# Cross-attention and feed-forward block: both halves of a pair's scores follow each other, one projection bank fewer and keys in the outputs' bank

## The reference, cut to what matters

```python
lat, ctx = layer_norm(latents, ...), layer_norm(context, ...)
q = (lat @ Wq)                                  # [b, heads, 256, 64]
k, v = jnp.split(ctx @ Wkv, 2, axis=-1)         # [b, heads, 512, 64]
k = apply_rope(k, cos, sin)
attn = softmax(clip(q @ k.T * scale, -11, 11))
x = x + (attn @ v) @ Wo + bo
# second layer, per token
att = softmax(q2 (16x8) @ k2.T / sqrt(8)); out = att @ v2
x = x + (out @ Wo + bo); h2 = rmsnorm(x)
x = x + sum over e of softmax(h2 @ Wg + bg)[e] * (h2 @ We[e])
```

## Time and profile before

| what | us |
|---|---|
| three runs | 311.20, 311.25, 309.62 (median 311.2) |
| the profiled execution's own time | 310.52 |
| its span | 308.7 |
| TensorE matmul busy | 293.3 (95%) |
| TensorE weight loads busy | 205.2 (66%) |
| VectorE busy | 247.7 (80%) |
| GpSimd busy | 207.4 (67%) |
| ScalarE busy | 162.2 (53%) |
| mean granted TensorE clock | 0.991 |

### The profile page before, as it was taken

The page is one execution under the profiler, slowest core; times in us unless marked ns, Lnnn a source line. Parts: engine busy times, 40 slices in busy tenths (PEclk is TensorE's granted clock), DMA queues, the critical chain, the costliest instruction groups (busy, mean ns, idle before and its releaser), DMA issues.

```text
span 308.7 us, 6625 instructions
## 1 busy us (share of the span) xinstructions
PE 293.3 (95%) x2482; PEld 205.2 (66%) x2482; DVE 247.7 (80%) x452; ACT 162.2 (53%) x324; POOL 207.4 (67%) x209
## 2 busy tenths in 40 slices
PE   6889998999999999999999999999999999999983
PEld 6777665766678767566777676566787665576651
DVE  1896999966775869899889788977857699887875
ACT  2447555568551745664615555784436468514632
POOL 7255784556465738777665777499927588878763
PEclk9799999999999999999999999999999999999998
DMA  7463422221111111111111012011101100000001
GB/s 197 160 181 92 123 57 53 61 62 36 36 45 25 35 36 34 36 37 33 37 36 34 19 35 53 8 45 36 29 22 37 36 18 2 0 19 0 1 2 34
DMA packets 16319, 14.24 MB, mean 46 GB/s; under 512 B 4832, under 2 KB 11808, under 8 KB 16288
## 3 DMA queue, kind: packets, MB, share of 16 engines
q1 hardware_dynamic: 14992, 13.49, 16.9%
q10 hardware_dynamic: 1296, 0.33, 0.5%
HBM read 4.89 MB, written 0.52 MB: 18 GB/s over the span
## 4 chain that ended last, share of the span: by engine, by line
PE 64%; DVE 11%; POOL 8%; ACT 5%; issue 5%; DMA 4%; SPq 2%; POOLq 0%; ACTq 0%; DVEq 0%
PE pv L659 13%; PE sc L643 13%; PE sums L680 6%; PE pj_k L581 5%; PE pj_k L583 4%; PE pj_k L582 4%; PE side L767 4%; POOL moe L1944 2%; PE side L843 2%; POOL e L1870 2%; DMA sin_in<-in_L_xattn_sin_dram 2%; DMA kswap<-ksin 2%; SPq L548 2%; PE side L688 2%; ACT e L963 2%
## 5 line engine op out<-in xcount | busy, mean ns | idle before, releaser
L1870 POOL TENSOR_SCALAR e<-e 128x1024 f32<-128x1024 f32 x64 | 70.9, 1108 | 56.9 <-ACT e L963 46.4
L963 ACT ACTIVATE e<-sc 128x1024 f32<-128x1024 f32 x64 | 65.6, 1025 | 32.1 <-PE sc L643 31.7
L643 PEld LDWEIGHTS sc<-qs,ks 64*128 64x128 f32 x768 | 49.6, 185 | 21.8 <-issue 18.3
L643 PE MATMUL sc<-qs,ks 64*128 64x256 f32 x768 | 62.5, 295 | 0.5 <-ACT e L963 0.3
L659 PE MATMUL pv<-e,v 128*64 128x256 f32 x496 | 60.4, 385 | 0.6 <-POOL e L1870 0.4
L1863 POOL TENSOR_TENSOR krot<-kcos,kswap 128x512 f32<-128x512 f32 x32 | 43.7, 1365 | 11.8 <-DMA kswap<-ksin 9.3
L659 PEld LDWEIGHTS pv<-e,v 128*64 128x64 f32 x496 | 32.8, 136 | 21.5 <-issue 4.5
L971 ACT ACTIVATE u<-pv 128x256 f32<-128x256 f32 x31 | 11.9, 385 | 54.0 <-PE pv L659 47.9
L1321 DVE TENSOR_TENSOR ks<-krot,ks 128x512 fp32r<-128x512 f32 x32 | 32.1, 1004 | 0.1
L1385 DVE TENSOR_TENSOR ksin<-pj_k,sinT 128x512 f32<-128x512 f32 x32 | 21.9, 685 | 4.0 <-PE pj_k L583 3.8
L955 ACT ACTIVATE v<-pj_k 128x512 f32<-128x512 f32 x28 | 16.8, 599 | 15.1 <-PE pj_k L583 14.7
(11 more groups left out here) (304 smaller groups left out, 575.5 us busy)
## 6 DMA issues: line engine op xcount, KB each, us to landing
kswap<-ksin SPq DMA_DIRECT2D x126, 64.0 KB, 2.0
ctx_in<-in_ctx_dram SPq DMA_DIRECT2D x4, 256.0 KB, 4.1
prod<-in_L_xattn_Wkv_dram SPq DMA_DIRECT2D x2, 512.0 KB, 7.0
x_in<-in_x_dram SPq DMA_DIRECT2D x1, 512.0 KB, 6.6
prod<-in_L_xattn_Wq_dram SPq DMA_DIRECT2D x1, 512.0 KB, 7.4
wo<-in_L_xattn_Wo_dram SPq DMA_DIRECT2D x1, 512.0 KB, 4.4
fwe<-in_L_ffn_We_dram SPq DMA_DIRECT2D x1, 512.0 KB, 4.3
out_dram<-x_in SPq DMA_DIRECT2D x3, 128.0 KB, 1.9
```

The source lines that it names most:

```text
L643: last = nc.tensor.matmul(sc[:, h, c * NT:(c + 1) * NT], ks[rows, j % 3, k_part, chunk], qs[rows, j % 2, q_part, :], start=(k_part + q_par ...
L963: nc.scalar.activation(e[:, j % 3, :, 2 * half:2 * half + 2, :].rearrange("p h c n -> p h (c n)"), sc[:, :, :], ACT.Exp, scale=SCALE).then ...
L1870: nc.gpsimd.tensor_scalar(a, a, EXP_HIGH, EXP_LOW, ALU.min, ALU.max).then_inc(s_clip, 1)
```

## The change

- Each half of scores has two banks of its own, sc0 and sc1. The banks of sc1 also hold the projections: value units in its first, queries in its second. Keys go to pv, the outputs' bank.
- TensorE's slot becomes: both halves of scores, d, sums, outputs of slot-1, a, queries of slot+2, one value unit, b, keys of slot+3, c.
- The waits follow the banks. The second half of scores waits for the value unit's copy and the low part of the queries of slot+1; outputs wait until `key_products` has read the keys of three pairs on; keys wait for the copy of the outputs; queries and value units wait for the second exponential.
- ScalarE: both exponentials, `key_hi(slot+1)`, output copy, `query_hi(slot+2)`, value copy.
- VectorE: `query_lo(slot+1)`, `key_products(slot+2)`, the steps, `key_lo(slot+1)`, the rest, both `add_chunks`.
- GpSimd: both clips, then `rotate(slot+2)`.
- norm0 moves to the new place "d", lat_T from slot 6 "a" to slot 5 "b" of a batch; value units are spread as one for a slot.

```diff
...
+QUERIES_AHEAD = 2
...
 POST_STEPS = {
-    (1, "a"): "norm0", (1, "b"): "norm1", (1, "c"): "norm2", (2, "a"): "norm3", (2, "b"): "out_proj",
+    (1, "d"): "norm0", (1, "b"): "norm1", (1, "c"): "norm2", (2, "a"): "norm3", (2, "b"): "out_proj",
     (3, "c"): "h_T", (4, "a"): "query_down", (4, "b"): "keyval2", (10, "c"): "o_T", (11, "a"): "out_proj2",
     (12, "c"): "h2_T", (13, "a"): "gate", (14, "b"): "moe0", (14, "c"): "moe1", (15, "b"): "moe2",
     (16, "a"): "moe3",
...
-PREP_STEPS = {(3, "b"): "ctx_T", (6, "a"): "lat_T"}
+PREP_STEPS = {(3, "b"): "ctx_T", (5, "b"): "lat_T"}
...
 def value_units(slot):
     b, p = divmod(slot, PAIRS)
     if slot <= 0:
-        return [2, 3] if slot == 0 else []
-    if p >= PAIRS - 2 and b + 1 < NB:
-        first = 8 * (b + 1) + 2 * (p - (PAIRS - 2))
-        return [first, first + 1]
-    if 1 <= p <= 4 and 0 <= b < NB:
-        return [8 * b + 3 + p]
-    return []
...
+        return []
+    if p >= 5:
+        return [8 * (b + 1) + p - 5] if b + 1 < NB else []
+    return [8 * b + 3 + p] if b < NB and (p or b) else []
...
-        sc = es.enter_context(nc.psum_tensor("sc", [128, 2, 512], fp32))
-        sc_bank = [sc[:, h, :] for h in range(2)]
+        sc = [es.enter_context(nc.psum_tensor(f"sc{half}", [128, 2, 512], fp32)) for half in range(2)]
+        sc_bank = [sc[0][:, h, :] for h in range(2)]
+        pj_k = [sc[1][:, h, :] for h in range(2)]
         own_bank = pb("own_bank")
-        pj_k = [pb(f"pj_k{i}") for i in range(2)]
...
         def value_bank(n):
-            return first_value_banks[n] if value_units_at_first(n) else pj_k[PLACE["values", n] % 2]
+            return first_value_banks[n] if n < SC else pj_k[0]
         def key_bank(j):
-            return pj_k[PLACE["keys", j] % 2]
+            return (pj_k[0], sc_bank[0], sum_bank, pj_k[0])[j] if j <= KEYS_AHEAD else pv_bank
         def query_bank(j):
-            return pj_k[PLACE["queries", j] % 2]
+            return own_bank if j == 1 else pj_k[1]
...
-                bank_free("keys", j)
+                if j == KEYS_AHEAD:
+                    pe.wait_ge(s_exp, 2)
+                elif j > KEYS_AHEAD:
+                    pe.wait_ge(s_u, j - KEYS_AHEAD)
                 split3(key_bank(j)[:, :], wkA[:, 0, cols], wkA[:, 1, cols], ctxT[:, b % 2, 0, :],
...
-                bank_free("queries", j)
+                if j >= QUERIES_AHEAD:
+                    pe.wait_ge(s_exp, 2 * (j - QUERIES_AHEAD) + 2)
...
-                if not value_units_at_first(n):
-                    bank_free("values", n)
+                if n == 1:
+                    pe.wait_ge(s_kmul, 6)
+                if n >= SC:
+                    pe.wait_ge(s_exp, 2 * slot + 2)
                 elif n >= 2:
                     pe.wait_ge(s_v, n - 1)
...
                 if half == 0:
                     pe.wait_ge(s_klo, j + 1)
                     pe.wait_ge(s_qlo, j + 1)
-                if j or half:
-                    pe.wait_ge(s_exp, 2 * j + half)
+                    if j:
+                        pe.wait_ge(s_exp, 2 * j - 1)
+                    else:
+                        pe.wait_ge(s_kmul, 4)
+                else:
+                    if j:
+                        pe.wait_ge(s_exp, 2 * j)
+                    if j == 1:
+                        pe.wait_ge(s_kmul, 2 * KEYS_AHEAD + 2)
+                    for n in value_units(j - 1):
+                        pe.wait_ge(s_v, n + 1)
+                    if j and j - 1 + QUERIES_AHEAD < NPAIR:
+                        pe.wait_ge(s_qlo, j + QUERIES_AHEAD)
...
+                if KEYS_AHEAD < j + KEYS_AHEAD < NPAIR:
+                    pe.wait_ge(s_kmul, 2 * (j + KEYS_AHEAD) + 2)
...
+            for slot in range(NPAIR - 2):
+                scores(slot, 0)
+                scores(slot, 1)
+                side_at(slot, "d")
...
+                if PAIRS < slot and slot % 2 == 0:
+                    sums(slot - 1)
+                times_values(slot - 1)
+                if slot <= PAIRS and slot % 2 == 0:
+                    sums(slot - 1)
+                side_at(slot, "a")
+                if slot + QUERIES_AHEAD < NPAIR:
+                    queries(slot + QUERIES_AHEAD)
+                for n in value_units(slot):
+                    values(n, slot)
+                side_at(slot, "b")
                 if slot + KEYS_AHEAD < NPAIR:
-                    if slot != 0:
-                        keys(slot + KEYS_AHEAD)
-                    if slot == 1 - KEYS_AHEAD:
-                        keep_busy(WARM_UP["lat_T"], pv_bank)
-                        side_product("lat_T", 0)
-                    if slot == -1:
-                        keep_busy(WARM_UP["queries"], pv_bank)
-                elif slot + 1 < NPAIR:
-                    queries(slot + 1)
-                side_at(slot - 1, "c")
-                if queries_ahead(slot):
-                    queries(slot + 1)
-                if slot == 0:
-                    keep_busy(WARM_UP["scores"], pv_bank)
-                if 0 <= slot < NPAIR:
-                    scores(slot, 0)
-                if slot == 0:
-                    keys(KEYS_AHEAD)
-                if not after_outputs(slot):
-                    side_at(slot, "a")
-                if 0 <= slot + 1 < NPAIR and slot + KEYS_AHEAD < NPAIR and not queries_ahead(slot):
-                    queries(slot + 1)
-                if PAIRS < slot <= NPAIR and slot % 2 == 0:
-                    sums(slot - 1)
-                if 1 <= slot <= NPAIR:
-                    times_values(slot - 1)
-                if 2 <= slot <= PAIRS and slot % 2 == 0:
-                    sums(slot - 1)
-                if after_outputs(slot):
-                    side_at(slot, "a")
-                if slot == 0:
-                    values(0)
-                    values(1)
-                if 0 <= slot < NPAIR:
-                    scores(slot, 1)
-                side_at(slot, "b")
-                for n in value_units(slot):
-                    values(n)
+                    keys(slot + KEYS_AHEAD)
+                side_at(slot, "c")
...
-            for slot in range(-KEYS_AHEAD, NPAIR - 2):
+            key_hi(0)
...
+            for slot in range(NPAIR - 2):
                 side_taken(slot - 1, "c")
-                if 0 <= slot < NPAIR:
-                    exps(slot, 0)
-                side_taken(slot, "a")
-                if 0 <= slot + 1 < NPAIR:
-                    query_hi(slot + 1)
-                if 1 <= slot <= NPAIR:
+                exps(slot, 0)
+                exps(slot, 1)
...
+                    key_hi(slot + 1)
                     attention_copy(slot - 1)
...
-                    exps(slot, 1)
...
+                side_taken(slot, "a")
+                if slot + QUERIES_AHEAD < NPAIR:
+                    query_hi(slot + QUERIES_AHEAD)
+                for n in value_units(slot):
+                    value_copy(n)
                 if slot < NPAIR - 3:
                     side_taken(slot, "b")
-                for n in units:
-                    value_copy(n)
-                if 0 <= slot + KV_AHEAD < NPAIR:
-                    key_hi(slot + KV_AHEAD)
...
-            for slot in range(-KEYS_AHEAD, AFTER):
...
+            for slot in range(AFTER):
...
-                if 1 <= slot <= PAIRS:
-                    add_chunks(slot - 1, 1)
-                side_taken(slot - 1, "c")
-                if 2 <= slot + KEYS_AHEAD < NPAIR:
-                    key_products(slot + KEYS_AHEAD)
...
+                if slot + 1 < NPAIR:
                     query_lo(slot + 1)
+                if slot and slot + 2 < NPAIR:
+                    key_products(slot + 2)
+                side_taken(slot - 1, "c")
                 if more and p == 6:
                     split_latT(b + 1)
-                if after_outputs(slot):
-                    side_taken(slot, "a")
-                if 1 <= slot + 1 < NPAIR:
+                if more and p == 4:
+                    split_ctxT(b + 1)
+                second_layer(slot, "first")
+                side_taken(slot, "d")
+                second_layer(slot, "early")
+                side_taken(slot, "a")
+                if slot + 1 < NPAIR:
                     key_lo(slot + 1)
...
-                if 0 <= slot < PAIRS:
-                    add_chunks(slot, 0)
+                if slot < PAIRS:
+                    for half in range(2):
+                        add_chunks(slot, half)
...
+            for slot in range(AFTER):
...
-                if 0 <= slot + KV_AHEAD < NPAIR:
-                    rotate(slot + KV_AHEAD)
                 second_layer(slot, -1)
-                if 0 <= slot < NPAIR:
+                if slot < NPAIR:
                     clip(slot, 0)
                 second_layer(slot, 0)
-                if 0 <= slot < NPAIR:
+                if slot < NPAIR:
                     clip(slot, 1)
+                if slot + KV_AHEAD < NPAIR:
+                    rotate(slot + KV_AHEAD)
...
```

118 lines of the change are left out of this document (48 added, 70 removed).

## The result

The changed kernel takes **354.28 us** (median of four runs, 350.59 to 357.52), the kernel before on the same chip 310.41 (308.76 to 311.25): ratio 1.138, 95% interval 1.134 to 1.143. The prediction was 324.5 with a range of 309 to 336: the direction was right, the loss is three times as large. The profiled execution of the changed kernel took 357.52 us, its span is 355.7; it is the slowest of the four, 3.2 above the median, so sums read from its trace come out somewhat high.

A forecast was written before the change was run, and what follows sets the result against it. TensorE was taken to set the pace, with VectorE's lag harmless. 310.5 + (208.4 work + 32 new stalls - 224.4 before) - 2 at the ends = 324.5 us, 4% slower, range 309 to 336.

The forecast's parts named there:

- the repricing: TensorE, slots 1 to 29: uninterrupted work recounted with fewer changes of tile shape, 217.2 us before and 208.4 after.
- stalls, slots 1 to 9: New waits from statistics, normalising and added chunks behind the low keys, and reciprocals behind later sums: 3.7 us.
- The gain: TensorE: fewer shape changes save 8.9 us in slots 1 to 29; slot 0 gives 0.9 and the end 1.1.
- the gain is missing: Rival: on TensorE the pause between shapes returns as a wait, 333 us; chance 0.19 together with the blocked case.
- The mechanism: Outputs wait for VectorE's key products and slip with its lateness; a slot lasts as long as the longer of both engines.
- nobody waits: Order before: VectorE lags several us in slots 13 to 15 and makes it up in 16 and 17, delaying nobody.
- the sum of the new waits: Slots 1 to 30: stalls estimated by groups of slots add up to 32 us.
- the paragraph on the clock: TensorE: a 2.5 us stall could halve the clock, costing about 1 us each; given no sum of its own.
- T+4.2, or x+3.5: End of VectorE's low keys, after slot start T, or by VectorE's lateness x if the second scores were late.
- blocked by GpSimd: Rival: GpSimd's second clip holds up VectorE's low keys, 8 us more, 332.5; chance 0.19 together with gain missing.
- faster: Rival: VectorE keeps up, so outputs hardly wait for key products; stalls under 17 us, 292.5 with none; chance 0.14.
- stalls two thirds: Rival: VectorE's instructions shorten and work behind the low keys fills idle time; 21 us of stalls, 313.5; chance 0.17.

The follow-up runs named there:

- e15: Changed kernel plus 6 to 17 unread dummy products on TensorE between the halves of scores in stalled slots, slot 1 excepted; 340.5 us, ratio 1.097.
- e5: Kernel before with VectorE's four sums of the second layer's products done twice in each of the first three batches; 321.5 us, ratio 1.038.
- e11: Kernel before with three idle VectorE reductions added at the end of each of slots 9, 17 and 25; 322.7 us, ratio 1.037.
- e17: e15 with GpSimd's second clip of each slot cut from 1024 to 16 columns; 337.9 us, ratio 1.090.
- e7: e1 with query_down, out_proj2 and gate moved to place d, directly behind the scores; 333.9 us, ratio 1.074.
- e8: e7 with norm3 also moved to d, and out_proj and keyval2 to a; 325.2 us, ratio 1.046.
- e1: Changed kernel with ScalarE's key_hi(slot+1) moved in front of both exponentials; 343.9 us, ratio 1.099.

## Why the prediction was wrong

By the slots' starts in the traces, against the lengths that the repricing gave each slot:

| term | predicted | e15 (clock kept up) | changed kernel |
|---|---|---|---|
| uninterrupted work, slots 1 to 29 | 208.4 | | |
| stalls, slots 1 to 9 | 3.7 | 12.9 | 13.4 |
| slots 12 to 16 | 8.2 | 11.5 | 14.0 |
| slots 17 to 19, 11, 27 | 4.1 | 5.6 | 5.1 |
| slots 20 to 24 | 9.2 | 12.9 | 22.0 |
| slots 25 to 30 without 27 | 6.8 | 8.4 | 13.0 |
| sum of stalls | 32 | 51 | 68 |

The lengths of the repricing are those of the slots before, less the changes of shape and the value units moved; besides slots 13 to 15 only their sum was on record. e15's 12.9 still holds the 1.7 us of half clock in slot 1. Together 308.7 - 2.0 (start) - 0.9 (slot 0) - 16.0 (208.4 for 224.4) + 67.6 - 1.6 (end without slot 30's stall) = 355.8, where the span is 355.7.

- **The gain held.** Slots of the changed kernel without a wait last 6.44 (4 and 6), 7.31 (14) and 11.19 us (10), where the repricing said 6.43 and 7.30, and 11.12 (11.51 before, less 0.39 for two changes). Slot 0 gave the 0.9, the end 1.6 for 1.1. The rival "the gain is missing" is out.
- **The mechanism held for the new order.** Outputs slip with VectorE's end: in slot 5 VectorE reaches the low queries at 57.02, 1.93 after T, and the outputs start at 58.77, 2.07 later than 1.61 after T. The low keys wait for ScalarE's (27.5 us). One detail differed: the profile names the low queries (29.1 us) and not kcos (1.7) as the releaser, since the second scores stand in front of the outputs. And the stalls came in half of slots 12 to 29 (nine), not in most. What did not hold is the premise on the order before, "nobody waits": e5 and e11 show that there too VectorE's lag is paid, where the side bank waits for it.
- **Two steps failed, and each alone would have left the range.** The larger is the sum of the new waits, 32 us: at full clock it was 49 to 51, and e15, with hardly any half clock, took 340.5 us. The other is the paragraph on the clock: it was given no sum and measured 13 to 16 us, which on 324.5 makes 337 to 341.
- **The clock**: "I give it no sum of its own", "each would cost about 1 us, a few of them". It was 13 stretches, 1.65 us for one in the pair of e11 and 13 to 16 us net for all by e15. The 1 us was a reading of too narrow a window: the earlier trace rows begin at 11, but that stretch begins at 9.8 and ends at 13.2 us (granted clock 0.50, 3.4 us), so it costs up to 1.7. The reason I gave for no sum, that no row shows it after so short a stall, was an absence of evidence: the trace before had no stalls. An upper end was at hand: 32 us of stalls in pieces of about 2 us make 16 of them, with the prediction's own 1 us each 16 us more, or 340. The Trainium skill (TensorE: Matmul & The Clock Gate, part 1) has idle TensorE lose half its clock; the traces of the changed kernel and of e11 agree that it falls at stalls, and show besides that an equal stall does not always bring it.
- **The size of the stalls** was 17 to 19 us too small, some 8 of it in slots 1 to 9. One term can be read off: the low keys were to end at T+4.2, or x+3.5. In each of slots 2 to 9 of the changed kernel they ended 0.6 to 1.4 us later than that, of which 0.43 to 0.89 is what the instruction took above its clean 0.68. The same lateness, 0.8, stands in slots 13 and 16. I had taken VectorE's rows at their clean lengths. VectorE in slots 4 and 5 of the changed kernel:

```profile
52.16 1.57 DVE L1289 TENSOR_TENSOR ks<-krot,ks 128x512 fp32r<-128x512 f32 x1 [0.98 <-ACT ks L912]
53.66 0.86 DVE L1294 BATCH_NORM_STATS2 c_stat<-ctx_in 128x6 f32<-128x128 f32 x4
...
55.50 1.60 DVE L1363 TENSOR_TENSOR moe<-e 128x512 f32<-128x512 f32 x2
57.02 0.41 DVE L1289 TENSOR_TENSOR qs<-sc,qs 128x256 fp32r<-128x256 f32 x1
```

and GpSimd beside it:

```profile
50.79 2.41 POOL L1837 TENSOR_SCALAR e<-e 128x1024 f32<-128x1024 f32 x2 [1.32 <-ACT e L935]
54.65 1.29 POOL L1830 TENSOR_TENSOR krot<-kcos,kswap 128x512 f32<-128x512 f32 x1 [1.46 <-issue]
```

The low keys start during the clips and last 1.57 us for 0.68, the added chunks start during the rotation and last 1.60 for 1.26 to 1.28: 1.2 of this slot's 1.9 us of lateness. That is the prediction's own rival "blocked by GpSimd", which I had priced at 8 us and kept out of the sum, with looking at the low keys alone. The Trainium skill (SBUF — State Buffer, on the engine side's ports) has the two engines exclude each other on a shared pair of ports; e17's rows, 1111 ns to 692, agree. How much of the 17 to 19 us it is in all stays open, as e17 can't tell. In sum VectorE's instructions did not become longer, its 323 of slots 1 to 29 took 182.6 us for 184.2 before; what counts is which of them is hit. Waits of VectorE for the side bank (dT 18.5 us, on 18.0) are in the same sum, and what e7 and e8 gained over e1 suggests that they weigh more.
- **The other rivals**: "faster" (under 17 us of stalls) and "stalls two thirds" were far off. The range lacked a case in which two of its bad cases come together with a third, the clock, that follows from stalls and is not independent of them.
